# Decoder layer: second attention's scores on array quarters, the next block's rows made in the rope stage, and six rope tiles ahead from the first step on

## The reference

```python
q_hk = (hidden_q @ Wq.T).reshape(Bv, Sv, H, K)                 # K = 128
q_big = jnp.einsum('bshk,hkq->bshq', q_hk, w_kc_q)             # 192 per head
q_big = _apply_rope(q_big, sin_q, cos_q)
kv_r = _apply_rope(kv_c, sin_k, cos_k)                         # the context, 64 x 64
q_r = jnp.einsum('bshq,hqr->bhsr', q_big, W_qr)
k_r = jnp.einsum('bld,hdr->bhlr', kv_r, W_kr)
scores = jnp.einsum('bhsr,bhlr->bhsl', q_r, k_r)
attn = jax.nn.softmax(scores, axis=-1)
ctx_c = jnp.einsum('bhsl,bld->bhsd', attn, kv_r)
ctx_lat = jnp.einsum('bhsd,hkd->bhsk', ctx_c, w_kc_kv)
return ctx @ Wo.T                                              # ctx is ctx_lat, heads side by side
```

## Time and profile before

| | |
|---|---|
| median of 3 runs | 767.41 us (766.45 to 767.72) |
| the profiled execution | 763.03 us |
| its span | 761.2 us |
| TensorE, VectorE, ScalarE, GpSimd busy in the span | 662.7, 529.0, 333.4, 237.2 us |

### The profile page before, as it was taken

The page is one execution under the profiler, slowest core; times in us unless marked ns, Lnnn a source line. Parts: engine busy times, 40 slices in busy tenths (PEclk is TensorE's granted clock), DMA queues, the critical chain, the costliest instruction groups (busy, mean ns, idle before and its releaser), DMA issues.

```text
span 761.2 us, 13640 instructions
## 1 busy us (share of the span) xinstructions
PE 662.7 (87%) x4850; PEld 490.5 (64%) x4850; DVE 529.0 (69%) x1237; ACT 333.4 (44%) x1001; POOL 237.2 (31%) x219
## 2 busy tenths in 40 slices
PE   4787999989999889989899898998979797899780
PEld 2465777767785557856578465785656586788660
DVE  4998789994676868578794777846587746344472
ACT  0477789986721173011730117301366354444340
POOL 1131000000028423453446534465334001201554
PEclk9997899996999999999999999999999999999995
DMA  8799800000000000000000100001071133333545
GB/s 302 162 382 420 351 2 2 1 2 1 2 15 15 1 1 1 1 14 1 16 21 23 55 1 15 22 21 43 14 251 50 48 93 97 117 105 100 155 127 179
DMA packets 49905, 61.44 MB, mean 81 GB/s; under 512 B 15536, under 2 KB 42416, under 8 KB 49584
## 3 DMA queue, kind: packets, MB, share of 16 engines
q1 hardware_dynamic: 45104, 50.88, 20.1%
q0 software_dynamic: 3072, 8.39, 3.6%
q10 hardware_dynamic: 1664, 1.31, 0.6%
HBM read 29.37 MB, written 31.20 MB: 80 GB/s over the span
## 4 chain that ended last, share of the span: by engine, by line
PE 65%; DVE 14%; ACT 9%; issue 6%; POOL 3%; DMA 2%; another core or an unknown queue 1%; ACTq 0%; POOLq 0%; DVEq 0%
PE bank L348 55%; PE bank L357 9%; DVE m L1052 3%; ACT ex L1546 2%; POOL r L1701 2%; ACT kbd L1425 1%; DVE qmax L1264 1%; DVE wlo L1296 1%; ACT vbd L1411 1%; DMA lncol<-in_L_attn_ln_kv_b 1%; DVE csum L1273 1%; POOL gb L1753 1%; ACT ex L1435 1%; ACT xth L1391 1%
## 5 line engine op out<-in xcount | busy, mean ns | idle before, releaser
L1052 DVE TENSOR_TENSOR m<-bank,cst 128x512 f32<-128x512 f32 x192 | 118.8, 682 | 47.0 <-PE bank L348 46.2
L1701 POOL TENSOR_TENSOR r<-m,m 128x512 f32<-128x512 f32 x72 | 91.3, 1291 | 134.9 <-DVE m L1052 123.0
L348 PE MATMUL bank<-xth,wbh 128*128 128x512 f32 x192 | 83.4, 434 | 4.1 <-DVE m L1052 4.1
L348 PE MATMUL bank<-xth,wbl 128*128 128x512 f32 x192 | 75.1, 391 | 0.0
L348 PE MATMUL bank<-xtl,wbh 128*128 128x512 f32 x192 | 75.1, 391 | 0.0
L1534 ACT ACTIVATE qc<-bank 128x512 f32<-128x512 f32 x32 | 17.4, 595 | 128.8 <-PE bank L348 128.8
L1546 ACT ACTIVATE ex<-bank,nmax 128x64 f32<-128x64 f32 x256 | 56.1, 346 | 27.2 <-DVE nmax L1267 27.0
L348 PE MATMUL bank<-r,wqk 64*64 64x512 f32 x512 | 61.1, 621 | 1.7 <-POOL r L1701 1.7
L1721 POOL TENSOR_TENSOR ex<-ex,inv 128x512 f32<-128x512 f32 x32 | 33.3, 1042 | 82.7 <-DVE inv L1276 82.5
L348 PE MATMUL bank<-wop,qc 128*128 128x256 f32 x256 | 58.0, 379 | 0.6 <-DVE qc L1281 0.6
L348 PEld LDWEIGHTS bank<-wop,qc 128*128 128x128 f32 x256 | 48.5, 190 | 11.4 <-issue 4.3
(11 more groups left out here) (218 smaller groups left out, 1553.4 us busy)
## 6 DMA issues: line engine op xcount, KB each, us to landing
slots<-cst SPq DMA_DIRECT2D x1, 13312.0 KB, 44.2
xs<-slots SPq DMA_DIRECT2D x46, 128.0 KB
slots<-ys SPq DMA_DIRECT2D x46, 128.0 KB
slots<-cst SPq DMA_DIRECT2D x1, 5120.0 KB, 49.7
wo_s<-in_L_xattn_Wo SPq DMA_DIRECT2D x1, 2048.0 KB, 18.3
wq_s<-in_L_xattn_Wq SPq DMA_DIRECT2D x1, 2048.0 KB, 11.9
wraw<-in_L_ffn_Wg SPq DMA_DIRECT2D x8, 256.0 KB, 5.0
wraw<-in_L_ffn_Wu SPq DMA_DIRECT2D x8, 256.0 KB, 5.3
```

The source lines that it names most:

```text
L348: return e.matmul(o, l, r, start=start, stop=stop, skip_group_check=True)
L1052: last = e.tensor_tensor(m4[n % 2][m][:, :].rearrange("p (b s) -> p b s", s=S), products[half][:, :].rearrange("p (b s) -> p b s", s=S), t ...
L1701: last = e.tensor_tensor(rope[n % 6][half][:, :], m4[n % 2][first][:, :], m4[n % 2][second][:, :], op)
```

## The change

The scores of one sequence are computed as 16 matmuls of 64 by 64 weights on the four quarters of the array, the even heads of each row pair into one bank and the odd into another (banks 4 and 5, or 2 and 3). For that the context's keys are needed untwinned: kvT replaces kvbd and kvbdT, and the context product becomes two matmuls on diagonal quarters, both into bank 7. The next block's rows are transposed at rope tiles 10 and 11 of the block before, in two portions, into a second pair of buffers. Tile 0 of the next block is made ahead of step 0, and tile s + 1 in step s, all in banks 0 and 1. The output tiles 0 to 2 are made in halves in steps 6 to 11, and tile 3 behind rope tile 6 of the next block. The router's transposes and logits come one tile later. VectorE now waits for each half of a rope tile by itself, and the order of its four products is changed.

```diff
-        AHEAD = {5: 0, 6: 1, 7: 2, 8: 3, 10: 4, 12: 5}
+        AHEAD = 6
-        ROUTE_AT = {"stats": 6, "norm": 7, "T": 8, "logits": 9, "max": 9, "exp": 10, "rank": 11, "pos": 12, "slots": 13}
+        ROUTE_AT = {"stats": 6, "norm": 7, "T": 9, "logits": 10, "max": 10, "exp": 11, "rank": 11, "pos": 12, "slots": 13}
-        out_bank = lambda blk, t: bank[4 + t % 2 if blk < 3 else t]
-        OUT_AT = [{9: 0, 10: 1, 11: 2, 12: 3}] * 3 + [{6: 0, 8: 1, 10: 2, 12: 3}]
+        out_bank = lambda blk, t: bank[(0, 1, 4, 5 if blk == 3 else 0)[t]]
+        OUT_AT = {6: 0, 8: 1, 10: 2}
...
-            odd = (n + (blk == 0)) % 2
-            return bank[odd], bank[2 + odd]
+            if blk == 0 and n < 3:
+                return bank[1], bank[3]
+            pair = 0 if blk and n < AHEAD else 2 * ((n + 1) % 2)
+            return bank[pair], bank[pair + 1]
+        def score_banks(b):
+            return (bank[2], bank[3]) if b % 2 else (bank[4], bank[5])
...
             def half_products(blk, n):
-                w.wait_ge(c_rm, 12 * blk + n - 1 if n > 1 else 12 * blk)
+                if blk and n < AHEAD:
+                    w.wait_ge(c_rm0, 12 * blk + n)
+                elif blk and n == AHEAD:
+                    w.wait_ge(s_ex, 32 + 8 * blk)
+                elif blk and n == AHEAD + 1:
+                    w.wait_ge(c_rm, 12 * blk + AHEAD)
+                    w.wait_ge(c_xc, 4 * blk)
+                else:
+                    w.wait_ge(c_rm, 12 * blk + n - 1 if n > 1 else 0)
                 for half in range(2):
+                    if half and blk and n < AHEAD:
+                        w.wait_ge(c_rm, 12 * blk + n)
...
-            def context_diag_T(blk, half):
-                transposes(e, [(bank[6][:, q * P:(q + 1) * P], kvbd[:, 4 * half + q, :]) for q in range(4)]).then_inc(c_kvTp, 1)
+            def context_T(blk):
+                for b in range(8):
+                    for c in range(2):
+                        last = mm(e, bank[6][64 * c:64 * c + 64, b * XC:(b + 1) * XC], kvr[0:64, b, :], ident[0:64, 0:64], True, True)
...
             def cross_scores(blk, b):
-                for n in range(NP):
-                    at = 64 * (n % 2)
-                    last = mm(e, bank[4 + b % 2][at:at + 64, (n // 2) * P:(n // 2 + 1) * P], qc[:, n, b * 64:(b + 1) * 64], kvbdT[:, b, :], True, True)
+                for n2 in range(4):
+                    if n2 == 3 or b:
+                        w.wait_ge(c_qb, 8 * (blk + 1))
+                    for odd in range(2):
+                        rows = slice(64 * odd, 64 * odd + 64)
+                        for c in range(2):
+                            last = mm(e, score_banks(b)[odd][64 * c:64 * c + 64, 64 * n2:64 * n2 + 64], qc[rows, 2 * n2 + c, b * 64:(b + 1) * 64],
+                                      kvT[rows, b, :], True, True)
...
             def contexts(blk, b):
-                mm(e, bank[7][:, :], kvbd[:, b, :], ssb[b % 2][:, :], True, True).then_inc(c_ctxv, 1)
+                for odd in range(2):
+                    rows = slice(64 * odd, 64 * odd + 64)
+                    last = mm(e, bank[7][rows, :], kvr[rows, b, :], ssb[b % 2][rows, :], True, True)
...
             for blk in range(4):
                 for n in rope_tiles(blk):
                     if blk or n > 2:
                         half_products(blk, n)
+                    if blk and n == AHEAD:
+                        for part in range(2):
+                            cross_out(blk - 1, 3, part)
+                    if n == 7:
+                        context_T(blk)
                     if blk:
                         route_step(blk - 1, n)
-                    if n in (9, 11):
-                        context_diag_T(blk, (n - 9) // 2)
+                    if n >= 10 and blk < 3:
+                        norm_T(blk, n - 10)
                     if n in LAT_AT[blk]:
                         latents(blk, LAT_AT[blk][n])
                 latents(blk, 3)
-                for s in range(13):
+                if blk < 3:
+                    half_products(blk + 1, 0)
+                for s in range(12):
                     if 3 <= s < 11:
                         cross_weights_T(blk, s - 3)
                     if s < 8:
                         cross_scores(blk, s)
                     if s == 1 and blk:
                         route_step(blk - 1, 12)
-                    if s < 4 and blk < 3:
-                        norm_T(blk, s)
-                    if 4 <= s < 12:
+                    if s >= 4:
                         contexts(blk, s - 4)
-                    if s in AHEAD and blk < 3:
-                        half_products(blk + 1, AHEAD[s])
-                    if s in OUT_AT[blk] and (blk, s) != (3, 12):
-                        cross_out(blk, OUT_AT[blk][s])
+                    if s < AHEAD - 1 and blk < 3:
+                        half_products(blk + 1, s + 1)
+                    if s >= 6:
+                        cross_out(blk, OUT_AT[s - s % 2], s % 2)
...
             def rope_products(blk, n):
-                w.wait_ge(c_proj, 24 * blk + 2 * n + 2)
-                for m, (half, q) in enumerate(((0, 0), (1, 1), (1, 2), (0, 3))):
+                for m, half, q in ((0, 0, 0), (3, 0, 3), (1, 1, 1), (2, 1, 2)):
+                    w.wait_ge(c_proj, 24 * blk + 2 * n + 1 + half)
...
+                    if m == 3:
+                        last.then_inc(c_rm0, 1)
```

More of the change, by code:

```diff
@@ L149, in decoder @@
         sem = lambda name: ctx.enter_context(nc.semaphore(name))
-        bank = [ctx.enter_context(nc.psum_tensor(f"bank{i}", [P, 512], F32)) for i in range(8)]
+        banks = ctx.enter_context(nc.psum_tensor("bank", [P, 8 * 512], F32))
+        bank = [banks[:, 512 * i:512 * i + 512] for i in range(8)]
         keep = Space(nc, 16512)
@@ L833, in tensor @@
             x_T(0)
-            cross_out(3, 3)
+            for part in range(2):
+                cross_out(3, 3, part)
             x_T(1)
@@ L1313, in vector @@
                 for s in range(13):
+                    if s < AHEAD and blk < 3:
+                        rope_products(blk + 1, s)
                     if s < 8:
@@ L1544, in cross_exp @@
                 w.wait_ge(s_exT, 32 + i - 3)
-                for h in range(8):
-                    last = e.activation(ex[b % 4][:, h * 64:(h + 1) * 64], bank[4 + b % 2][:, h * 64:(h + 1) * 64], ACT.Exp,
-                                        bias=nmax[b % 2][:, h:h + 1], scale=1.0)
+                for odd in range(2):
+                    for n in range(4):
+                        last = e.activation(ex[b % 4][:, (2 * n + odd) * 64:(2 * n + odd + 1) * 64], score_banks(b)[odd][:, n * 64:(n + 1) * 64], ACT.Exp,
+                                            bias=nmax[b % 2][:, 4 * odd + n:4 * odd + n + 1], scale=1.0)
                 last.then_inc(s_ex, 1)
@@ L1591, in scalar @@
                 for s in range(13):
-                    if 1 <= s < 5 and blk < 3:
-                        norm_T(blk, s - 1)
                     if 3 <= s < 11:
@@ L1682, in context @@
                 e.tensor_tensor(kvr[:, :, :], kvr[:, :, :], kvt[:, :, :], ALU.add).then_inc(c_kvr, 1)
-            def context_diag(blk):
-                w.wait_ge(c_kvr, blk + 1)
-                w.wait_ge(s_S, 16)
-                w.wait_ge(c_ctxv, 8 * blk)
-                w.wait_ge(c_kvTp, 2 * blk)
-                for h2 in range(2):
-                    last = e.tensor_tensor(kvbd[:, :, 64 * h2:64 * h2 + 64], kvr[:, :, :],
-                                           C("half")[:, h2:h2 + 1].rearrange("p (o d) -> p o d", o=1).broadcast_to([P, 8, XC]), ALU.mult)
-                last.then_inc(c_kvbd, 1)
             def rope_sums(blk, n):
```

144 lines of the change are left out of this document (75 added, 69 removed).

## The result

| | before | after |
|---|---|---|
| median, measured side by side | 767.57 us (766.45 to 770.49, 4 runs) | 747.72 us (745.28 to 750.69, 4 runs) |
| the profiled execution | 763.03 us | 745.28 us |
| its span | 761.2 us | 743.5 us |

The ratio is 0.9737, with a 95% interval from 0.9693 to 0.9782: 20.2 us less, between 16.7 and 23.6 (the two medians are 19.9 apart). The prediction was 745 us, in a range from 736 to 761.

The account below looks back on a forecast made before the run. TensorE's own work was taken to bound a whole period, with about 6 us idle. Gains of 19.6 us in the periods and 3.0 in block 0 and the last block made 22.6, so 745 us against the median, range 736 to 761.

Parts of the forecast that it names:

- The periods: Three periods of the second attention, 93.0, 95.7 and 95.6 us before: predicted gains 5.9, 6.9 and 6.8, total 19.6.
- block 0: Block 0's rope stage: 1.5 us gained, between 0 and 3, as its statistics come a tile earlier.
- the last block: The last block's attention: 1.5 us gained (0 to 3) from shorter scores and evenly spread output halves.
- The rope stage: Part of a period after the steps: 39.9 us on TensorE, with no wait unless rope tile 11 is late.
- The steps: Steps 0 to 11 of a period: end at 48.9 us, waits 4.3 in all, VectorE bounding steps 2 to 5.
- the router's slots 1.7: VectorE's router slots, in the early steps of later periods: priced at 1.7 us.
- The router: Transposes moved from rope tile 8 to 9: the 2.54 us mxhat wait goes, and 1.6 of clock in two periods.
- Scores and contexts: TensorE's matmuls in the steps: a score 0.60 us instead of 1.02, a context 0.96 instead of 0.86.
- The rival of serial quarters: A context's two quarters run one after the other, 1.8 us each context: 768, no change; chance 0.06.
- GpSimd falling behind: Rival: GpSimd's step takes 7 instead of 4.8 us over steps 4 to 9: 778; chance 0.07.
- Longer steps: Rival: every VectorE step up to tile 5 takes 0.5 us longer, by handoffs or GpSimd waits: 754; chance 0.22.
- The clock: The 0.50 clock behind the router's mxhat wait in two of three periods: 1.6 us each, to go.

Follow-up runs that it names:

- `after_again`: The changed kernel, unaltered, run once more beside the other kernels of its set on one chip: 733.34 us, ratio 0.9774 to the kernel before.
- `after_slots_late`: Changed kernel with the router's slots, all but their first instruction, moved from step 2 to step 6, scatters to steps 7 to 10: 742.96 us, ratio 0.9681.
- the third set: Third group of follow-up kernels, run on one chip, five rounds each, with the kernel before in between; that kernel took 750.77 us there.
- the early work: Changed kernel with one added VectorE reduction of 0.65 us at the end of steps 1, 2 and 3 of blocks 0 to 2: 733.97 us, ratio 0.9783.

## Why the prediction was right, and where it was off

**The total and its parts.** 22.6 us were predicted and 20.2 measured, 17.8 of them in the attention sum (17.4 and 17.3 with `after_again`). The periods gave 12.9 for 19.6, block 0 2.0 for 1.5, the last block 3.0 for 1.5. So the total came out better than its largest part, of which a third did not come: 2.0 more at the two ends and the 2.4 by which the time gained more than the attention sum covered for it, and that was luck. Block 0's gain has another cause than the one named, statistics a tile earlier: with the half-wise wait undone its rope stage takes what it took before the change. Of the last block's 3.0, 0.9 is a wait that the prediction did not count, and no run takes the rest apart.

**The rope stage** was counted at 39.9 and took 39.6, 39.6 and 38.8 in the three periods. The third has no transposes of next rows in it, which the sum had not left out.

**The steps** are where it was off. They were to end 47.2 us after the last latents in the first period and 48.9 in the others. They ended after 48.7, 52.9 and 51.8. In the second period the 4.0 are the wait before tile 4, 2.67 for 1.8, the clock behind it, 2.4 on tile 4 and 0.5 on the transposes, and about 1 of small terms, less 0.8 at the copy of context 1, 0.44 for 1.25. In the third they are that wait, two waits for the copy, 1.39 and 0.56 for 1.25, and small terms, as output halves of 1.83 for 1.73. The 1.5 of the first period, which has no slots, are such terms and a wait of 1.85 for the copy; no run separates them. The step of the prediction that failed is "the router's slots 1.7": they took 2.72 (and 3.88 in one of `after_again`'s two periods). The price was read where GpSimd had one scaling beside them, and applied where it has its scaling and two sums back to back. `after_slots_late` confirms it: with all but the slots' first instruction out of these steps, no wait is left before tile 4, and the periods are 88.4, 88.4 and 87.5. For a period without slots the schedule had 87.1, so what is then missing is 1.3, 1.3 and 0.4.

**The router** was right: TensorE no longer waits for mxhat. The line alone gave the 2.5, and in two periods the 1.6 of clock, that the sum had, less the wait of 1.27 that comes with leaving the keys where they were. Undone in the changed kernel it cost 3.9 in one rope stage, 2.3 in another and nothing in the third.

**Scores and contexts** were right in size: 0.51 to 0.63 for 0.60, and 0.97 to 1.01 for 0.96. Between the two nearest rows the right one was the one with the same 64 columns and the narrower weights. Of the scores' gain only a part reaches the period, as the prediction said of the first five. The Trainium skill, TensorEngine Tiling (Array Packing), section Instruction Overhead, would have had 0.8 for the scores if the records came one after another, as the prediction's estimate had it; the trace does not agree, with 32 records in 0.51 on four quarters.

**The rival of serial quarters** is rejected: two quarters with different rows in one bank took 0.97 for 512 columns each, not 1.8. The Trainium skill, TensorEngine Tiling (Array Packing), Gotcha 1: PSUM Pressure, keeps different row tiles out of one bank at the same time; no run here shows a delay from it where the two write to different partitions.

**GpSimd falling behind** is rejected too: no wait of TensorE in the periods is put down to it. It acted through VectorE, which stood behind it. **Longer steps**, which named waits for GpSimd as a cause, is what happened in part, in one step and by 1.0 (or 2.2), not in every step by 0.5.

**The clock** was counted only as a gain, after the router's wait. The same price stood behind a wait of 1.8 that the prediction kept, and it was paid there in some periods. In the sum it should have been a term with a chance of its own.

**The half-wise waits** had no price of their own in the prediction; undone, they cost 6.6 us in time and 10 to 13 in the attention sum. The schedule had them in, but it did not say that so much of the gain rests on them.

**Not taken apart:** no run has the early rope tiles, the moved rows or the output halves alone. Their share is known only as what the sum leaves them.

## What to carry to other kernels

When work is moved into a stretch in which another engine shares its path to SBUF, take its price from a row where that engine was busy, and not from the quiet place it comes from. A wait of TensorE can have two prices, its length and what the granted clock takes behind it (here with waits of 1.6 to 3.8 us); the second comes in some executions and not in others, so compare kernels stage by stage and let several executions speak. Where an engine passes tiles on to one that is nearly as busy, handing over halves can be worth more than half as much as all the reordering around it (6.6 us against 10.9 in the third set).

## What the runs showed of the hardware

**VectorE's small operations wait for GpSimd's work on SBUF.** In the slots above the cast took 0.90, begun inside GpSimd's sums, and 0.17 in `after_slots_late`, begun after GpSimd's scaling had ended; the reductions between (0.29 for two) are not stretched though they lie inside the sums too. The negation went from 0.66 to 0.17 when the early work moved it out of the sums. The longest case is a negation in the third period of the changed kernel, VectorE's timeline and then GpSimd's:

```profile
475.03 2.52 DVE L1314 TENSOR_SCALAR nmax<-qmax 128x8 f32<-128x8 f32 x1
```

```profile
475.02 2.49 POOL L1738 TENSOR_TENSOR r<-m,m 128x512 f32<-128x512 f32 x2
```

It starts 0.01 after GpSimd's sums and ends 0.04 after them (477.55 and 477.51): it stood still as long as they ran. The Trainium skill, SBUF — State Buffer, section Who interferes with whom, states just this: VectorE and GpSimd take a shared pair of ports as a lock, the later one stands still until the other is through, VectorE needs the pair for two SBUF inputs or in a two-port mode, which casts and operations with a scalar can enter, and its reductions on this chip never do. The traces agree on the instructions. In all 14 of them the 18 casts of `index` that began inside a GpSimd tensor operation took 0.90 to 0.95, against 0.17 for the others, and ended 0.03 after it; of over 400 reductions begun so none was stretched; and `pick`, with two inputs in SBUF, is the instruction of the 3.88 us above. Of GpSimd standing still behind VectorE they have no long case.

**The clock's fall is not tied to one length of wait.** After the same wait of 2.67 us before tile 4 it stood at 0.50 for 6.8 us in the second period and stayed at 1.00 in the third; in `after_again` a wait of 2.64 left it at 1.00, and one of 3.83 came with 6.8 us at 0.50. Of all 14 traces, the falls inside the periods came with waits of 1.64 to 3.84 us, while the waits of 1.77 and 1.79 in `after_slots_late` had none.
